# A decoder layer's first stage: context batch by batch, shorter lags, distances kept in SBUF

## What is computed

```python
# attention without softmax, one head of 16 repeated 16 times, then the projection
q, k, v = split(x @ qkv_w.T + qkv_b)
out = tile(where(tril, q @ k.T, 0) @ v, 16) @ proj_w.T + proj_b
x = layernorm(x + out)
# alignment: distances of every context row to every row of x, a cheapest path through them
D = sqrt(max(|ctx|^2 + |x|^2 - 2 ctx @ x.T, 0))          # 77 x 256 per batch
R[i, j] = D[i, j] + min(R[i-1, j], R[i, j-1], R[i-1, j-1])
x = layernorm(x + expanded)   # expanded[j] = sum of the ctx rows that the path pairs with j
# feed forward: product-key lookup, top 8 of 64 twice, gather, gelu, gate
x = layernorm(x + ffn(x))
```

## Time and profile before

| what | us |
|---|---|
| median of 3 runs | 2913.27 (2911.16 to 2913.49) |
| the profiled execution | 2914.01 |
| its span, first to last instruction | 2912.3 |
| TensorE busy in it | 2655.0 (91%) |
| VectorE busy | 2215.0 (76%) |
| ScalarE busy | 734.8 (25%) |
| GpSimd busy | 885.7 (30%) |
| mean granted clock of TensorE | 0.954 |

### The profile page before, as it was taken

How to read it: one execution, slowest core, us unless ns; L and a number is a source line. 1 busy time by engine, 2 the same in 40 slices (tenths; PEclk the granted TensorE clock), 3 DMA queues, 4 the chain that set the end, 5 groups by cost and what they waited for, 6 DMA issues and landing times.

```text
span 2912.3 us, 104477 instructions
## 1 busy us (share of the span) xinstructions
PE 2655.0 (91%) x43108; PEld 2296.1 (79%) x43108; DVE 2215.0 (76%) x7510; ACT 734.8 (25%) x1275; POOL 885.7 (30%) x702
## 2 busy tenths in 40 slices
PE   6961168799999999999999999999999999999996
PEld 5851155788888888888888888888888888888895
DVE  5668966877777777777777777777777788877754
ACT  4740023322222222222222222222222222222210
POOL 1330164233323332333233323332333333333332
PEclk9985579999999999999999999999999999999997
DMA  5550337300000000000000000000000000000000
GB/s 170 173 158 28 65 112 182 66 13 14 13 14 11 12 11 14 10 13 13 14 14 14 13 14 14 14 13 14 14 14 13 14 14 14 14 14 13 10 10 12
DMA packets 84639, 99.52 MB, mean 34 GB/s; under 512 B 6189, under 2 KB 74702, under 8 KB 84046
## 3 DMA queue, kind: packets, MB, share of 16 engines
q1 hardware_dynamic: 84190, 92.94, 11.5%
HBM read 65.13 MB, written 27.79 MB: 32 GB/s over the span
## 4 chain that ended last, share of the span: by engine, by line
PE 81%; issue 1%; DVE 1%; ACT 0%; POOL 0%; DVEq 0%; ACTq 0%; POOLq 0%
PE bank L1052 32%; PE bank L1086 31%; PE bank L1070 9%; PE bank L1023 8%; PE bank L1038 1%; PE bank L1010 1%; DVE hot L1269 0%; DVE shared L1281 0%; POOL hot L989 0%; ACT L1171 0%; ACT gelh L1171 0%; ACT x2T L1152 0%; DVEq L1290 0%; ACT xnT L1144 0%; DVE yo L1303 0%
## 5 line engine op out<-in xcount | busy, mean ns | idle before, releaser
L989 POOL TENSOR_TENSOR hot<-hot,valsT 128x512 f32<-128x512 f32 x512 | 733.3, 1451 | 1663.0 <-DVE hot L1269 1663.0
L1052 PE MATMUL bank<-x2T,shared 128*64 128x128 f32 x16384 | 952.3, 274 | 1.6 <-ACT gelh L1171 1.4
L1052 PEld LDWEIGHTS bank<-x2T,shared 128*64 128x64 f32 x16384 | 890.6, 137 | 23.7 <-issue 9.0
L1269 DVE TENSOR_TENSOR hot<-places,valsT 128x1024 f32<-128x1024 f32 x512 | 653.8, 1317 | 0.2 <-issue 0.2
L1086 PE MATMUL bank<-up,shared 64*128 64x256 f32 x4096 | 449.0, 378 | 1.5 <-DVE shared L1281 1.5
L1086 PE MATMUL bank<-up,gelh 64*128 64x256 f32 x4096 | 446.4, 377 | 0.0
L1086 PEld LDWEIGHTS bank<-up,shared 64*128 64x128 f32 x4096 | 396.8, 188 | 58.8 <-issue 11.4
L1086 PEld LDWEIGHTS bank<-up,gelh 64*128 64x128 f32 x4096 | 395.2, 187 | 56.2 <-issue 11.5
L1070 PE MATMUL bank<-hot 64*64 64x64 f32 x16384 | 303.9, 224 | 33.2 <-POOL hot L989 17.0
L1070 PEld LDWEIGHTS bank<-hot 64*64 64x64 f32 x16384 | 268.7, 137 | 82.0 <-issue 82.0
L1281 DVE TENSOR_TENSOR shared<-bank,shared 128x512 f32<-128x512 f32 x256 | 164.7, 685 | 176.7 <-PE bank L1070 176.3
(11 more groups left out here) (149 smaller groups left out, 2167.0 us busy)
## 6 DMA issues: line engine op xcount, KB each, us to landing
x_scratch<-x_sb SPq DMA_DIRECT2D x64, 256.0 KB, 2.1
xT_sb<-in_xT SPq DMA_DIRECT2D x32, 256.0 KB, 2.9
x_sb<-in_x SPq DMA_DIRECT2D x32, 256.0 KB, 2.9
x_again<-x_scratch SPq DMA_DIRECT2D x32, 256.0 KB, 2.8
x_tile<-x_scratch SPq DMA_DIRECT2D x32, 256.0 KB, 3.7
up<-in_table SPq DMA_DIRECT2D x2, 4096.0 KB, 36.6
yo<-x_scratch SPq DMA_DIRECT2D x32, 256.0 KB, 2.8
out_y<-yo SPq DMA_DIRECT2D x32, 256.0 KB, 2.1
```

Source lines behind the costliest of these rows:

```text
L989: pool.tensor_tensor(lo, lo, valsT[:, par, 2, TQ * q:TQ * (q + 1), None].to_broadcast([P, TQ, NK]), ALU.mult).then_inc(gated_ready, 1)
L1052: mm = pe.matmul(ps_h[q % 2][half(c), i, :], dnT[:, k, lo // 2, half(lo % 2)], x2T[:, par, k, c, :], start=(k == 0), stop=(k == CC - 1))
L1269: dve.tensor_tensor(hot[:, q % SLOTS], places[:, None, None, :].to_broadcast([P, 2, TQ, NK]), valsT[:, par, 0:2, TQ * q:TQ * (q + 1), None ...
```

## The change

It touches the first stage and the table's load. In the diff's order:

- `dist_d` in HBM and its four loads are gone. `store_dist` writes the square roots from SBUF into `cost`, which lies in SBUF from the start, in four DMAs of 20 rows (20 KB) each.
- The context comes batch by batch: `load_ctx` issues two DMAs (77 rows of 1 KB; 256 pieces of 77 numbers), with two buffers for the columns. From batch 2 on it waits for two semaphores: `norm_seen`, which VectorE raises when it has come to `norms` of the batch two earlier, and `ctxm2_ready`, raised by `ctx_scale` of the batch two earlier.
- `norms` squares one batch a step, by another instruction; the reduction in `setup` is cut in two halves, in steps 0 and 1.
- The lags are 0 to 6 and every list has another order; ScalarE's `qkv` is split in `qk` and `v`. SyncE's steps are all written out, without a loop.
- At the start xT of batch 0 is loaded ahead of the weights, two memsets move forward with a semaphore of their own (`pads`), and ScalarE runs one square root ahead of everything.

```diff
                 def load_xT(b, par):
-                    if isinstance(b, int) and b == 1:
-                        sp.wait_ge(consts, 1)
...
-                    if isinstance(b, int) and 2 <= b < 2 + NB // 8:
-                        some = slice(8 * (b - 2), 8 * (b - 1))
...
+                def load_ctx(b, par):
+                    if later(b, 2):
+                        sp.wait_ge(norm_seen, b - 1)
+                        sp.wait_ge(ctxm2_ready, b - 1)
+                    sp.dma_start(ctx_rows[:, b, :], ctx_rows_d[b]).then_inc(rows_in[par], 16)
+                    sp.dma_start(ctx_cols[:, :, par, :], ctx_cols_d[:, b].rearrange("(k p) s -> p k s", k=CC))\
+                        .then_inc(cols_in[par], 16)
+
                 def store_dist(b, par):
                     sp.wait_ge(root_ready, b + 1)
-                    sp.dma_start(dist_d[bass.ds(b, 1)].rearrange("a (i j) -> (a i) j", i=RP),
-                                 dist_sb[:, par]).then_inc(dist_out[par], 16)
+                    for g in range(NG):
+                        sp.dma_start(cost[NB * g + b:NB * g + b + 1, :].rearrange("a (r t) -> a r t", t=T),
+                                     dist_sb[RG * g:RG * (g + 1), par, :]).then_inc(dist_out[par], 16)
...
-                pipeline(sp, [(load_xT, 0), (load_x, 5), (store_x1, 7), (store_dist, 10)], 12)
+                load_xT(1, 1)
+                sp.wait_ge(pads, 1)
...
+                for i in range(1, NB + 6):
+                    for stage, lag, first in ((load_xT, 0, 2), (load_x, 1, 0), (store_x1, 4, 0), (load_ctx, 2, 0),
+                                              (store_dist, 6, 0)):
+                        if first <= i - lag < NB:
+                            stage(i - lag, (i - lag) % 2)
...
-                pipeline(pe, [(head, 2), (qkv, 0), (wei, 1), (turn_v, 1), (attn, 3), (turn_x1, 6), (dist, 7)], 10)
+                pipeline(pe, [(qkv, 0), (head, 1), (dist, 4), (wei, 0), (turn_v, 0), (attn, 1), (turn_x1, 2)], 6)
...
-                pipeline(act, [(root, 9), (head, 2), (qkv, 0), (wei_off, 1), (ctx_scale, 6), (x1_cols, 6), (std, 4)], 12)
+                pipeline(act, [(qk, 0), (std, 2), (v, 0), (head, 1), (wei_off, 0), (ctx_scale, 3), (root, 4), (x1_cols, 2)], 6)
...
                 def dist(b, par):
                     dve.wait_ge(dist_mm, b + 1)
                     if later(b, 2):
-                        dve.wait_ge(dist_out[par], dmas(b, par) - 16)
+                        dve.wait_ge(dist_out[par], NG * (dmas(b, par) - 16))
...
                 def norms(b, par):
...
+                    dve.wait_ge(rows_in[par], dmas(b, par))
+                    rest(dve, norm_seen)
...
+                pipeline(dve, [(recip, 2), (dist, 4), (settle, None), (scale, 2), (wei_diag, 0), (v, 0), (setup, 0),
+                               (residual, 1), (norms, 3), (settle, None), (stats, 1), (settle, None), (aggr, 1)], 6)
...
-                for g in range(NG):
-                    sp.dma_start(cost[NB * g:NB * (g + 1), :], dist_d[:, RG * T * g:RG * T * (g + 1)])\
-                        .then_inc(cost_in[g], 16)
```

More of the change, by code:

```diff
@@ L81, in decoder_layer @@
         dn = shared[:, DN:].rearrange("p (j c) -> p j c", c=C)
+        cost = shared[:, 0:RG * T]
         w_in = sem("w_in")
         wq_in = sem("wq_in")
-        ctx_in = [sem(f"ctx_in{i}") for i in range(NB // 8)]
+        rows_in = [sem(f"rows_in{i}") for i in range(2)]
+        cols_in = [sem(f"cols_in{i}") for i in range(2)]
+        norm_seen = sem("norm_seen")
+        pads = sem("pads")
         consts = sem("consts")
@@ L118, in decoder_layer @@
         dist_out = [sem(f"dist_out{i}") for i in range(2)]
-        cost_in = [sem(f"cost_in{g}") for g in range(NG)]
         table_init = sem("table_init")
@@ L317, in _ @@
                 pool.memset(wqkv[:, :, GAP + HS:2 * GAP], 0.0)
+                pool.memset(proj[:, :], 0.0)
+                pool.memset(eps_col[:, :], EPS)
+                pool.drain()
+                pool.nop().then_inc(pads, 1)
                 pool.memset(ones[:, :], 1.0)
@@ L361, in turn_v @@
                     pe.wait_ge(vT_ready, b + 1)
+                    if not later(b, 1):
+                        pe.wait_ge(consts, 1)
                     if later(b, 1):
@@ L432, in qkv, with v @@
                         .then_inc(qk_ready, 1)
+                def v(b, par):
                     if later(b, 2):
@@ L452, in ctx_scale @@
                 def ctx_scale(b, par):
-                    if not later(b, 1):
-                        for part in ctx_in:
-                            act.wait_ge(part, 32)
+                    act.wait_ge(cols_in[par], dmas(b, par))
                     if later(b, 2):
@@ L536, in norms @@
                 def norms(b, par):
-                    if isinstance(b, int) and b < NB // 8:
-                        dve.wait_ge(ctx_in[b], 32)
-                        for k in range(8 * b, 8 * b + 8):
-                            dve.tensor_tensor_reduce(out=sq_scr[:, k % 8, :], in0=ctx_rows[:, k, :],
-                                                     in1=ctx_rows[:, k, :], scale=1.0, scalar=0.0, op0=ALU.mult,
-                                                     op1=ALU.add, accum_out=ctx_norm[0:S2, k:k + 1])
-                def setup(b, par):
+                    dve.wait_ge(rows_in[par], dmas(b, par))
+                    rest(dve, norm_seen)
+                    rows = ctx_rows[:, bass.ds(b, 1), :].rearrange("s a c -> s (a c)")
+                    dve.scalar_tensor_tensor(out=sq_scr[:, :], in0=rows, scalar=1.0, in1=rows, op0=ALU.mult, op1=ALU.mult,
+                                             accum_out=ctx_norm[0:S2, bass.ds(b, 1)])
+                def setup(b, par):
+                    if not later(b, 2):
+                        dve.wait_ge(p_in, 64)
+                        some = slice(P * b, P * (b + 1))
+                        dve.tensor_reduce(proj[0:HS, some], projT[:, :].rearrange("d (c h) -> d c h", h=NHEAD)[:, some],
+                                          AX.X, ALU.add).then_inc(setup_v, 1)
                     if not later(b, 1):
-                        dve.wait_ge(p_in, 64)
-                        dve.tensor_reduce(proj[0:HS, :], projT[:, :].rearrange("d (c h) -> d c h", h=NHEAD), AX.X,
-                                          ALU.add).then_inc(setup_v, 1)
                         dve.tensor_copy(iota[:, :], iota_i[:, :])
@@ L647, in _ @@
                 pool.drain()
+                pool.nop().then_inc(table_init, 1)
                 short = S2 - RG * (NG - 1)
```

36 lines of the change are left out of this document (14 added, 22 removed).

## The result

| | before | changed |
|---|---|---|
| median, us | 2913.22 | 2987.55 |
| profiled execution (span) | 2914.0 (2912.3) | 2986.0 (2984.3) |
| search's first instruction, us | 208.64 | 282.28 |
| release of the context load, first and last turn, us | | 39.88 and 261.00 |
| a batch in the steady first stage, us | 4.99 | 8.2 |

The change made the kernel slower, ratio 1.0259 with a 95% interval of 1.0247 to 1.0272. The forecast had the sign and the place, and under half of the size: 28 us of 74. The measured time lies above the forecast range, which ended at 2964 us. The whole loss is in the first stage: the search starts 73.6 us later and the span is 72.0 longer.

A forecast was written before the change was run, and what follows sets the result against it. TensorE's pace bounded the first stage, VectorE's search the second; the change shifts the search: 41 + 180.9 + 13.5 + 1.1 = 236.5 against 208.64, so 2913.3 + 28 = 2941 us, range 2912 to 2964.

The forecast's parts named there:

- the ring: Through SyncE's queue: distance step waits for stores behind the context load, which waits for the previous distance step; 6.7 us a turn.
- the start: First stage's beginning: first product about 5.9 us, reduction halves from about 11.5 and until about 18, step 5 at 35.4.
- distance step to release: VectorE's distance step to the context load's release: 2.4 us through ScalarE, 2.56 through VectorE's residual; the later counts, 2.55.
- first release that binds: First context-load release that sets the pace, after step 5: 35.4 + 3.0 + 2.55, so at 41 us.
- last release to the search: End of the first stage: 13.5 us from step 32's release until the last stores land, then 1.1 to the search.
- the price of the store: Four distance stores in SyncE's queue: 0.41 us an issue, 1.23 for three, and 1.98 from the fourth's issue to VectorE.
- a single store: In SyncE's queue, one distance store instead of four: a turn of 5.5 us, the sum 32 us lower, faster than before.
- Rival (a): Stores into SBUF land sooner than into HBM, so turns are faster, down to 2909 us; chance 0.12 of 5.8 or less.
- The second ring: SyncE's xT load stands behind the four stores: 11.0 us in two steps, 5.5 each, limiting any gain to 2909 us.
- Rival (b): First stage: TensorE stays the bound, with a turn under 4.99 us; 18 us earlier, 2895 us; chance 0.05.
- Rival (c): TensorE, idle 1.7 us a step, falls to its low clock level: 8.1 us a turn, 2979 us; chance 0.06.
- The handover: Between the stages: without the table's load through HBM the search is released sooner, 5.3 us saved.

The follow-up runs named there:

- e1: Changed kernel with the distance stores ahead of the context load in SyncE's step, nothing else: 2914.0 us, ratio to before 1.0001.
- e3: Changed kernel with four SBUF buffers for the distances instead of two, order as changed: 2952.0 us (one run).
- e2: Changed kernel with distances going to HBM in one store and back in four loads, order as changed: 2908.1 us, ratio to before 0.9982.
- e5: Changed kernel with one store of 80 rows into the table's four partitions instead of four stores, order as changed: 2961.9 us, ratio to before 1.0165.
- e4: Changed kernel with its four stores of 20 rows going to HBM, four loads in the second stage, order as changed: 2925.6 us (one run).
- e6: Changed kernel with one distance store to HBM, four loads back, and the store ahead of the context load: 2904.8 us, ratio to before 0.9967.
- e8: Changed kernel with one 80-row store into the table in SBUF, placed ahead of the context load: 2901.8 us, ratio to before 0.9961.

## Why the prediction was right, and where it was wrong

**Right:** that the change closes a ring, context load, stores, distance step, and context load again, and that it and not TensorE sets the pace; e1 opens it at one place (the order) and e3 at another (the buffers); VectorE's wait for the store nearly goes in e1, with the whole loss, and goes in e3. Right too: the start, to 1.1 us, and the time from distance step to release, 2.55 and 2.46 by turns for 2.55. That the latter agrees so closely is luck in part: the forecast had two ways, 2.4 through ScalarE and 2.56 through VectorE's residual, and took the later. The one through ScalarE releases the load and takes 0.1 more than forecast, and the residual isn't in the ring, since VectorE's semaphore comes 1.4 us after the distance step (129.52).

| term | forecast | measured |
|---|---|---|
| first release that binds | 41 | 39.9 |
| distance step to release | 2.55 | 2.55 |
| two context issues | 0.92 | 0.80 |
| from store issue to store issue, three times | 0.41 | 0.79 |
| last store's issue to VectorE | 1.98 | 2.56 |
| one turn | 6.7 | 8.2 |
| 27 turns (the last is 6.6) | 180.9 | 221.1 |
| last release to the search | 14.6 | 21.3 |
| search starts | 236.5 | 282.3 |

**The step that failed** is the price of the store, in the sentence that took 0.41 us an issue from rows of other transfers, and 1.98 us of landing from the one row of a store to HBM. Measured were 0.79 and 2.56: three times 0.38 and once 0.58 is 1.7 us a turn, less 0.12 for the context and 0.05 for VectorE's part. That is 1.55 for each of 26 turns of 8.25 us; the 27th, in whose step no batch's scores are left for ScalarE to wait for, is 6.6 and so 0.1 shorter than forecast; together 40.2 us. The end of the stage adds 6.7 more. Of these 1.6 lie in the first four stores and their landing (release to distance step 5.7 for 4.1) and 2.0 behind the last root (6.0 for 4.0, in which the last four stores stand); the other 3.1 lie between them, where TensorE is busy for 10.2 of 20 us and at its low level (distances in 1.97 us for 1.03). 40.2 + 6.7 - 1.1 at the start is the 45.8 us by which the search was later than forecast.

The prediction also said that with a single store the turn would be 5.5 us. That holds for one store to HBM (e2, 5.43) and not for one into the table (e5, 7.46): the landing was taken to be the same for both.

**The range failed** for two reasons. An issue was bounded by 0.36 to 0.46, the spread of the rows at hand, none of which puts twenty rows into one partition; that no row has a store from SBUF into SBUF was said of the landing and not of the issue. And the upper end took one bad case at a time, a slow landing (7.6) or a slow scaling (7.5), where both unknown prices belonged to one unknown transfer and came together.

**Rival (a)** went the wrong way: VectorE sees the same 20 rows 1.51 us after their issue in HBM (e4) and 2.56 in one partition of SBUF. By the rule of the Trainium skill's "DMA: Bandwidth & Descriptors", section "Anatomy of one DMA", which is on transfers that GpSimd issues, HBM is the slowest target; measured here, issued by SyncE, it was the faster one for this shape, and the measurement decides. The second ring which (a) named is real (e3, 6.46 us). Rival (b) didn't occur; e6 and e8 come near it (5.24 us) with another order. **Rival (c)**, the clock, is in part true: from 47 to 254 us TensorE waited over 2 us for x1 in 15 steps, and the granted level fell behind 11 of these waits and not behind the other four, nor behind any of the 11 waits of 1.2 to 1.8 us; the mean was 0.91. Its price, 8.1 us a turn and 2979 us, lies nearer to the measured 8.2 and 2988 than the forecast does, and that is chance. The turn is the same with and without a low stretch (8.27 and 8.25 us), and VectorE's idle time is put down to the store. In the turn with the low stretch TensorE has the next distances ready at 134.86, 1.5 us before VectorE starts on them, and in the next one at 141.53, 3.1 before (144.58). The rival's sum is also off in itself: it stretches the 3.0 us to 5.6 and then adds 5.9; with 5.6 it is 7.8 a turn.

The rule of the Trainium skill's "DMA: Bandwidth & Descriptors", "Rules for kernel authors", that small transfers are to be put together, holds for the issues: e5 saves 2.5 us of them. The landing went the other way; for this one store it grew from 2.56 to 3.8 or more.

The handover was forecast at 5.3 us less. e6 and e8 differ in the destination alone and show it: in e6, through HBM, the second stage begins at 192.99 and the search at 198.62, 5.63 us on; in e8, through SBUF, at 194.29 and 194.92, 0.63 on. Of these 5.0 us the later end of the last store takes back 1.3, so the search comes 3.7 earlier. In the changed kernel this gain is there too and lies under the 73.6 us by which the search starts later.

The start, from the timeline, with the two halves of the reduction and batch 0's projection behind them, to be held against the earlier trace rows: forecast 5.9, 11.5 and 18, measured 5.40, 10.70 and 17.2 (14.96 + 2.26).

```profile
5.40 1.96 PE L368 MATMUL bank<-xT_sb,wqkv 128*80 128x256 f32 x4 [5.40 <-DMA bias<-in_bqkv]
...
10.70 2.26 DVE L564 TENSOR_REDUCE proj<-projT 16x128 f32<-16x2048 f32 x1
...
14.96 2.26 DVE L564 TENSOR_REDUCE proj<-projT 16x128 f32<-16x2048 f32 x1
...
17.37 2.04 PE L408 MATMUL bank<-proj,headT 128*128 128x256 f32 x4 [2.67 <-DVE proj L564]
```

## What to carry to other kernels

When a change gives an in-order queue a new wait, write down the loop: who raises the semaphore, what stands behind the waiting instruction in the queue, and whether that comes back to the one who raises it. The loop's length is the period, however idle every engine looks. Here moving one entry gave back 73 us and two more buffers 36 (one run), where making the transfer itself better (e5) won 26. Price a transfer only by a row with the same shape on both sides, destination partitions included, and when no such row exists let its unknown prices go to their bad ends together.

## What the runs showed of the hardware that was not expected

- A store of 20 rows of 1 KB from 20 partitions into one partition of SBUF holds SyncE's queue for 0.72 us (718 to 888 ns, 128 times), 0.79 from issue to issue; the same rows to HBM 0.33 and 0.40 (e4). Into four partitions, 80 rows take 0.56 (e5). No run stores 20 rows into 20 partitions of SBUF, so whether it is SBUF or the one partition that is dear isn't shown.
- Such a store is seen by VectorE 2.56 us after its issue, where HBM takes 1.51; the store of 80 rows into four partitions takes 3.78 to 4.51 in the rows above, 3.7 to 5.1 over 16 batches. I have no run that tells why.
- A landing isn't a property of the shape alone. The same store of 80 rows to HBM lands after 1.9 us in e2, where it stands behind the two context issues, and after 3.3 in e6, where it stands right behind the loads of xT and x and the store of x1 (medians, in this order):

```profile
dist_scratch<-dist_sb SPq DMA_DIRECT2D x32, 80.0 KB, 1.9
...
dist_scratch<-dist_sb SPq DMA_DIRECT2D x32, 80.0 KB, 3.3
```

- The median landings of x and xT are 4.0 and 3.8 us in e5, for 2.9 before. That the store into four partitions holds them up isn't shown: they are 3.7 and 3.5 in e2, which stores to HBM, and 3.5 and 3.3 in e8, which makes the same store.
